# Two graph layers on one core: dense products moved ahead of the neighbour sums, and a new interleaving on TensorE

## What is computed

```python
# layer 0 (h = relu(layernorm(x)))
type_sum = adj @ h
attn_a = sigmoid([type_sum, h] @ Wa.T + ba);  attn_b = sigmoid([type_sum, h] @ Wb.T + bb)
g = h @ W_sa
scores = (g @ a_sa[:256])[:, None] + (g @ a_sa[256:])[None, :]
e = where(adj != 0, exp(-leaky_relu(scores, 0.01)), 0)
x_a = (e / (e.sum(1) + 1e-5)) @ g
x_b = adj @ (h @ W_g) + b_g
x = x + sigmoid(attn_a * x_a + attn_b * x_b)
# layer 1 (h = relu(layernorm(x)), deg = row sums of adj)
pooled = (adj + I) @ h / deg + h
x = x + relu(pooled @ W1 + b1)
```

## Time and profile before

| | |
|---|---|
| runs of the kernel before | 670.83, 672.12, 672.31 us, median 672.12 |
| the profiled execution, its span from first to last instruction | 671.5 us |
| PE busy | 625.2 us (93 %), 5488 matmuls |
| DVE busy | 470.2 us (70 %) |
| ACT busy | 327.2 us (49 %) |
| POOL busy | 89.8 us (13 %) |
| DMA | 74.85 MB, mean 111 GB/s |

### The profile page before, as it was taken

The page is one execution under the profiler, slowest core; times in us unless marked ns, Lnnn a source line. Parts: engine busy times, 40 slices in busy tenths (PEclk is TensorE's granted clock), DMA queues, the critical chain, the costliest instruction groups (busy, mean ns, idle before and its releaser), DMA issues.

```text
span 671.5 us, 15005 instructions
## 1 busy us (share of the span) xinstructions
PE 625.2 (93%) x5488; PEld 544.5 (81%) x5488; DVE 470.2 (70%) x1147; ACT 327.2 (49%) x748; POOL 89.8 (13%) x146
## 2 busy tenths in 40 slices
PE   2289999969999999999999999999989999999994
PEld 1168888858888888888888888888878888888883
DVE  4498889998888989898989899998153234223332
ACT  2168696858576758495857667585020000000000
POOL 4122110202020201102020205010010001000100
PEclk9979999989999999999999999999999999999997
DMA  6945034808080716263544526221134545554441
GB/s 151 230 131 77 1 115 91 204 1 204 0 203 38 165 76 127 102 101 111 92 129 74 149 54 157 46 102 51 51 100 115 155 149 156 147 158 136 147 132 31
DMA packets 28462, 74.85 MB, mean 111 GB/s; under 512 B 3870, under 2 KB 18458, under 8 KB 26777
## 3 DMA queue, kind: packets, MB, share of 16 engines
q1 hardware_dynamic: 11202, 48.24, 21.6%
q0 software_dynamic: 14272, 22.14, 19.5%
q10 hardware_dynamic: 2967, 4.20, 2.7%
HBM read 71.15 MB, written 25.56 MB: 144 GB/s over the span
## 4 chain that ended last, share of the span: by engine, by line
PE 67%; issue 9%; DVE 7%; ACT 1%; POOL 1%; ACTq 0%; DVEq 0%; POOLq 0%
PE accA L576 10%; PE accA L577 10%; PE accA L570 8%; PE accA L571 8%; PE accE L586 8%; PE accE L588 8%; PE accE L587 8%; DVE Z L854 3%; DVE E L861 2%; PE dA L595 1%; PE dA L597 1%; PE dA L596 1%; PE tp L562 1%; PE dB L595 1%; PE dB L597 1%
## 5 line engine op out<-in xcount | busy, mean ns | idle before, releaser
L586 PE MATMUL accE<-h,Z 128*128 128x257 f16 x676 | 185.7, 275 | 0.4 <-DVE E L861 0.4
L588 PE MATMUL accE<-h,E 128*128 128x257 f16 x676 | 184.9, 273 | 0.0
L587 PE MATMUL accE<-h,Z 128*128 128x256 f16 x676 | 184.3, 273 | 0.0
L854 DVE SCALAR_TENSOR_TENSOR Z<-adjT,vr,Z 128x256 f32<-128x256 bf16 x338 | 147.8, 481 | 21.0 <-ACT Z L413 18.8
L570 PE MATMUL accA<-adjT,h 128*128 128x256 bf16 x676 | 157.4, 277 | 0.0
L571 PE MATMUL accA<-adjT,h 128*128 128x256 bf16 x676 | 157.3, 277 | 0.0
L576 PE MATMUL accA<-h,adjT 128*128 128x257 f16 x676 | 149.8, 273 | 1.9 <-DVE wm L1086 1.1
L408 ACT ACTIVATE Z<-slp,sr 128x256 f32<-128x256 f32 x338 | 150.3, 496 | 2.4 <-PE accE L588 1.1
L577 PE MATMUL accA<-h,adjT 128*128 128x256 f16 x676 | 149.8, 273 | 0.0
L861 DVE TENSOR_TENSOR E<-Z 128x512 bf16<-128x512 f32 x169 | 115.0, 686 | 0.5
L413 ACT ACTIVATE Z<-Z 128x512 f32<-128x512 f32 x169 | 102.9, 617 | 0.0
(11 more groups left out here) (114 smaller groups left out, 628.4 us busy)
## 6 DMA issues: line engine op xcount, KB each, us to landing
adjT_store<-adjT SPq DMA_DIRECT2D x13, 1664.0 KB, 5.4
stage<-in_adj_dram POOLq DMA_DIRECT2D x36, 416.0 KB, 6.9
adjT<-adjT_store SPq DMA_DIRECT2D x26, 512.0 KB, 4.6
adjT<-adjT_store SPq DMA_DIRECT2D x13, 640.0 KB, 3.9
stage<-in_adj_dram POOLq DMA_DIRECT2D x12, 415.5 KB, 9.7
out_dram<-osb ACTq DMA_DIRECT2D x12, 256.0 KB
xs<-in_x_dram SPq DMA_DIRECT2D x5, 256.0 KB, 11.6
xs<-in_x_dram SPq DMA_DIRECT2D x3, 320.0 KB
```

Of the source, the lines that this page charges most:

```text
L586: pe.matmul(accE[e][:, 0:D + 1], zhi, h1[0][:, t, 0:D + 1], start=(t == 0), stop=False)
L587: pe.matmul(accE[e][:, 0:D], zhi, h2[0][:, t, :], start=False, stop=False)
L588: ins = pe.matmul(accE[e][:, 0:D + 1], zlo, h1[0][:, t, 0:D + 1], start=False, stop=(t == TILES - 1))
L854: ins = dve.scalar_tensor_tensor(out=Z[:, u, v], in0=rows, scalar=vr[:, t:t + 1], in1=Z[:, u, v], op0=ALU.mult, op1=ALU.mult)
```

## The change

Three things are changed together.

1. The dense products of layer 0 are made once, in the prologue, for all rows (`dense`, a 512-column product with `W_sa` and `W_g` side by side, into the two banks of `dn`), and kept in `HI` and `LO`. Units then sum `g` itself, and the adjacency product sums `h @ W_g` plus two gate columns. Likewise `dense1` makes `h @ W1` of a pair as soon as its layer norm is there, and layer 1 only sums. The weights now have to be there before the first of these products.
2. Results come out row by row, with the adjacency as weights in both layers. `turn_e`, `turn_p` and the splitting of their results are gone. What is turned is only `h`, for the dense products.
3. The adjacency product of pair m+1 is spread over the units of pair m, in 13 pieces of 8 matmuls: one after each unit from unit 3 on, the last three after unit 12. For this there are two buffers `adjT`, turned in three chunks; `Z` and `E2` shrink from 13 buffers to a ring of 6. Layer 1 begins with the last two pairs, whose adjacency is still there.

POOL takes over the bias, the addition to `x` and the gate columns. No loop is left: all code is straight.

```diff
-        adjT = sb("adjT", [P, PAIRS, 2, P, 2], BF16)
-        Z = sb("Z", [P, PAIRS, 2, 2 * P])
+    RING = 6
+        adjT = [sb(f"adjT{k}", [P, PAIRS, 2, P, 2], BF16) for k in range(2)]
+        Z = sb("Z", [P, RING, 2, 2 * P])
...
+            def dense(i):
+                if i == 0:
+                    pe.wait_ge(wlo_ok, 2)
+                pe.wait_ge(hTl_ok, i + 1)
+                for e in range(2):
+                    if i >= 1:
+                        pe.wait_ge(lo_ok, 2 * i - 1 + e)
...
+            def unit(m, u):
+                n = m * PAIRS + u
+                pe.wait_ge(e2_ok, n + 1)
...
+                if u == 0 and m >= 1:
+                    pe.wait_ge(wm_ok, 2 * m)
...
+            for m in range(1, LAST):
+                for u in range(PAIRS):
+                    unit(m, u)
+                    if u >= 3:
+                        neighbours(m + 1, u - 3)
+                    if u == 10:
+                        turn1(m - 1)
+                    if u == 12:
+                        dense1(m - 1)
+                for u in range(PAIRS - 3, PAIRS):
+                    neighbours(m + 1, u)
...
+            def leaky(m, u):
...
+                if n >= RING:
+                    act.wait_ge(unit_done, n - RING + 1)
...
+            def first_halves1(m):
+                act.wait_ge(dn1_ps, m + 1)
...
+                    if u < PAIRS:
+                        leaky(m, u)
+                    if u >= 1:
+                        expo(m, u - 1)
+                    if u == 2 and m >= 2:
+                        turned1(m - 2)
+                    if u == 4 and m >= 2:
+                        first_halves1(m - 2)
+                    if u == 7:
+                        half_tanh(m - 1)
...
+                    if u == 2 and m >= 2:
+                        turned_second1(m - 2)
+                    if u == 4 and m >= 2:
+                        second_halves1(m - 2)
+                    if u == 5:
+                        row_sums(m - 1)
...
+                    mask(m, u)
+                    split(m, u)
+                    if m + 2 < PAIRS and u in (6, 10, 12):
+                        turn_adj(m + 2, {6: 0, 10: 1, 12: 2}[u])
...
+            def with_bias(m):
...
+                for e in range(2):
+                    ins = pool.tensor_scalar(wm[:, e], bgrep[:], gate[:, e, 1:2], None, ALU.mult)
...
+                pool.tensor_tensor(wm[:], wm[:], ub[:], ALU.add).then_inc(bg_ok, 1)
+            def residual(m):
...
+                pool.tensor_tensor(xs[:, tiles], xs[:, tiles], wx[:], ALU.add).then_inc(x1_ok, 1)
```

More of the change, by code:

```diff
@@ L453, in _ @@
-            act.wait_ge(sl_ok, PAIRS)
-            def sums_out(m, h, first=False):
-                act.wait_ge(a_done, 2 * m + (h + 1))
-                if h == 0 and not first:
-                    act.wait_ge(db_ok, m)
-                act.activation(Ta[:, 0, h], accA[h][:, 0:2 * P], ACT.Copy).then_inc(th_ok, 1)
-            def attn_out(q):
-                act.wait_ge(rs_ok, q + 1)
-                for e in range(2):
-                    act.activation(AE[:, e], accE[e][:, 0:D], ACT.Copy, scale=rs[:, e:e + 1]).then_inc(ae_ok, 1)
@@ new lines, in _ @@
+            norm(0)
+            norm(1)
+            turned(0)
+            first_weights(0)
+            first_weights(1)
+            for s in range(PAIRS + 5):
+                if s + 1 < PAIRS:
+                    turned(s + 1)
+                if s + 2 < PAIRS:
+                    norm(s + 2)
+                if s < PAIRS:
+                    scores(s)
+                if 0 <= s - 4 < PAIRS:
+                    expo(0, s - 4)
+                if s < PAIRS:
+                    first_halves(s)
+                    left(s)
+                if 0 <= s - 3 < PAIRS:
+                    leaky(0, s - 3)
+                if s == 5:
+                    first_weights(2)
@@ L557, in _ @@
+            for k in range(PAIRS):
+                store_out(k)
+            act.wait_ge(o_out[0], out_count(LAST, 0))
+            act.wait_ge(o_out[1], out_count(LAST, 1))
         @block.tensor
@@ new lines, in _ @@
+                for u in range(PAIRS - 3, PAIRS):
+                    neighbours(m + 1, u)
+            for u in range(PAIRS):
+                unit(LAST, u)
+                if u >= 2:
+                    pooled(0, u - 2)
+                if u == 10:
+                    turn1(LAST - 1)
+                if u == 12:
+                    dense1(LAST - 1)
+            for u in range(4):
+                pooled(1, u)
+            pooled(0, LAST - 1)
+            for u in range(4, 10):
+                pooled(1, u)
@@ L794, in _ @@
+            turn1(LAST)
+            for u in range(10, LAST):
+                pooled(1, u)
+            dense1(LAST)
+            for u in range(3):
+                pooled(2, u)
+            pooled(0, LAST)
+            pooled(1, LAST)
+            for u in range(3, PAIRS):
+                pooled(2, u)
+            for k in range(3, PAIRS):
+                for u in range(PAIRS):
+                    pooled(k, u)
         @block.vector
@@ L1136 @@
+            for k in range(PAIRS):
+                output(k)
 _INS = ['x', 'adj', 'L0_gnn_W_sa', 'L0_gnn_a_sa', 'L0_gnn_W_gcnb', 'L0_gnn_b_gcnb', 'L0_gnn_Wa', 'L0_gnn_ba',
```

1504 lines of the change are left out of this document (709 added, 795 removed).

## The result

| | before | changed |
|---|---|---|
| median of 4 runs (lowest to highest) | 672.21 us (670.83 to 674.5) | 708.21 us (704.54 to 710.76) |
| ratio, 95 % interval | | 1.052 (1.049 to 1.055) |
| profiled span | 671.5 us | 706.3 us |
| PE / DVE / ACT / POOL busy | 625 / 470 / 327 / 90 us | 621 / 480 / 316 / 272 us |

A forecast was written before the change was run, and what follows sets the result against it. PE, without holes in steady pairs, bounds the kernel; its work falls, but holes, DVE's path and a long prologue outweigh that. 134.7 + 369 + 28.6 + 140.1 + 9.1 = 681.5 us of span, so 682 us; range 658 to 702.

The forecast's parts named there:

- unit 0 of pair 1 starts: End of the prologue and pair 0: the first unit of pair 1 starts at 134.7 us.
- pairs 1 to 11: Layer 0 pairs: ten of 33.6 us and one of 32.9, 369 us in all (ends 362 and 385).
- pair 12, layer 1, tail: Last layer 0 pair 28.6 us, the rest of layer 1 140.1, last output chain and end of span 9.1.
- the hole of 2.5 us: Before unit 0 of each next pair, PE stands still 2.5 us: a chain of 5.1, of which 2.6 is covered.
- DVE's path as what decides the steady pair: In steady layer 0 pairs, DVE's path with POOL's blocking takes 33.5 us and decides, against 32.9 over PE.
- steps 5 to 11: Prologue: 6.6 us a step on PE, seven steps, 46 us (45 to 50).
- moving one call would not end the hole: Pause between pairs: counted from the last unit instead of `dense1`, the chain gives the same 2.5 us.
- the hole before unit 0 of pair 1, counted as above: First boundary, between pairs 0 and 1: the steady pair's chain with only 8 matmuls as cover, 3.7 us.
- steps 0 to 4: Prologue: 4.8 us a step, plus 3 for a cold first product and 4 for `W1` scale and transposes: 31 us.
- 33.6 us a pair: Period of a steady layer 0 pair: DVE's path of 33.5 us with a little for semaphores; ends 32.9 and 35.
- POOL's share: In each layer 0 pair, POOL's additions and products stop DVE for 2.8 us.
- The clock rival: The granted clock falls in the 12 holes between pairs, 1.6 us each, 19 us: 701 us; chance 0.15.

The follow-up runs named there:

- experiment 7: POOL's bias product and two additions cut to 8 of 256 columns, against the changed kernel with first boundary reordered, row sums earlier, splits behind the next mask: 655.1 us.
- experiment 2: Row sums of the pair before put ahead of layer 1's second halves and the mask of unit 4, from pair 2 on, against the changed kernel: 679.83 us.
- Experiment 1: Gates of pair 0 and last transposes of pair 2 moved from before pair 1 to inside it, against the changed kernel: 697.63 us.
- Experiment 8: Against the changed kernel reordered (667.54 us), each alone: smaller prologue batches 659.14; pair 9's load issues later 664.96; bias product on ACT 666.74. All three: 655.35 us.
- experiment 3: POOL's bias product, its addition and the addition to x cut to 8 of 256 columns, against the changed kernel: 710.4 us.
- experiments 4 and 5: First: ring of 8 instead of 6, against the changed kernel, 704.65 us. Second: that plus 22 unused matmuls in the pause of pairs 1 to 11, 691.85 us.

## Why the prediction was wrong

By its own terms, which sum to 681.5 us of span against 706.3:

| term | forecast | measured | off |
|---|---|---|---|
| unit 0 of pair 1 starts | 134.7 | 147.7 | +13.0 |
| pairs 1 to 11 | 369 | 380.5 | +11.5 |
| pair 12, layer 1, tail | 177.8 | 178.1 | +0.3 |

**Right.** PE's rates and its own 30.4 us a pair (30.3 when nothing else binds, experiment 7); the hole of 2.5 us and every link of its chain; DVE's path as what decides the steady pair; layer 1 and the tail; steps 5 to 11 (47.1 for 46), and what follows up to the first hole (28.6 for 29). The start of `dense(0)` (24.20 for 25) is luck in part, since it lay between 21.0 and 27.1 in the traces. The sentence that moving one call would not end the hole holds only for a call that leaves the row sums behind unit 4: experiment 2 moved them past both.

**Failed: "the hole before unit 0 of pair 1, counted as above", 3.7 us.** It was 9.93. The chain was copied from the steady pair, where ACT and DVE have masked four units ahead while PE finishes. At this boundary DVE's list has two items in front, `gates(0)` and `turn_adj(2, 2)`, that wait for the end of pair 0. Experiment 1 takes just these away, with the two calls of ACT that go with them, and finds 3.80. This is 6.2 of the first +13, about half.

**Mis-sized: steps 0 to 4, "4.8 us a step".** They took 37.9 us, not 31, the other half of the first +13: `dense(5)` started at 62.08, not 56. The time of a step was taken from `dn`'s banks. What set step 2, 9.2 us, was the inverse deviations of four pairs at once, whose statistics stood on DVE behind earlier dense products; with such pauses the clock was granted at 0.81 to 0.85 between 30 and 60 us. Experiment 8 gives back 6.0 us in the trace (8.4 between the medians).

**Mis-sized: 33.6 us a pair.** 34.1 in the steady ones. This small +0.5 hides two errors that nearly cancel, which is luck. Mask and split stand 1.51 us apart instead of 1.40, since a split right behind its own mask waits for it: +1.1 in the ten units of DVE's path. POOL's share was put at 2.8 us, all on masks and splits; DVE is busy 479.6 us in the changed kernel and 456.7 in experiment 3, so it was 1.8 a pair, more than half of it on `eg`: -1.0. (POOL itself works longer than forecast: its additions take 1.28 and 1.39 us in the mean instead of 1.11, its two products 0.97 each instead of 0.3. The 1.11 was the one addition with a float16 input; the twelve in float32 took 1.07.) The remaining 0.4 us is not assigned.

**Missing: pair 9, +4.5.** POOL's queue was not walked for the one pair whose load has 12 DMAs a chunk. Experiment 8 moves the issues, and pairs 9 and 10 together get 3.0 us shorter. Pair 1 (+2.4, half clock behind the first hole) and pair 11 (+1.6, the same) make up most of the rest.

**The clock rival** got 0.15 at 19 us. In the changed kernel it hit 1 of 11 steady holes. But experiments 4 and 5 show it as real and near: it takes 13 us once the period is 33.0 instead of 34.1. It stood as a separate case where it should have been a widening of the range.

## What to carry to other kernels

Walk each engine's list separately at the first and the last turn of a loop: what is free in the steady turn because others run ahead may be a full stop there, and here one such stop, 9.9 us, was as long as four steady holes. Where two items in an in-order list do not depend on each other, put the one that the busiest engine waits for first, even if it feels like the later one: moving one call gave 26 to 28 of 36 us. Before taking work off a second engine, fill the pauses of the first, since relief elsewhere can turn into a slower clock.

## What the runs showed of the hardware

- The same pause of 2.5 us on PE let the granted clock fall behind 1, 8 or 9 of 11 such pauses, depending on the kernel around it (periods of 34.1, and of 33.0). What in the rhythm decides was not tried.
- A DVE operation on 128x4 float32 with one tensor input (`eg`) takes 0.15 to 0.22 us, up to 0.35 beside POOL's issue of DMAs, and 2.0 to 2.15 when a POOL addition of 128x512 follows within 0.7 us (7 of 13 pairs of the changed kernel). One on 128x2 with two inputs (`nmr`) takes 0.11 to 0.16 us, and 1.05 when it starts 0.24 us behind the start of such an addition. The Trainium skill, in "SBUF — State Buffer", section "Who interferes with whom", has `tensor_scalar` among the operations that can take the port pair that DVE shares with GpSimd, and says that whoever issues first gets it. The first half fits these rows. The second half can't be read from recorded starts: `nmr`, which started second, waited for the addition, but `eg`, which started first by the record, also ended only with it (268.92 and 268.88). Which of the two took the ports first in that case, no run shows.
- On POOL, an issue of one DMA takes about 0.55 to 0.65 us (12 in 6.57, 4 in 2.39; 0.65 in the mean of 144).
